# FFN weights loaded one pair of heads earlier, turned behind the last denominators and kept in SBUF; the first layer norm's scaling on ScalarE

## The chip, the core and the metric

The kernel runs on one core of a Trainium2 chip. The metric is the device time of one launch in microseconds. The engines are PE (matmuls), DVE (vector), ACT (scalar), POOL (GpSimd) and SP, whose queue issues all DMAs here. Each engine works through its own list of instructions in order and waits on semaphores.

## The reference

The input is x of 2 batches x 2048 rows x 256. All arithmetic is fp32.

```
x = x + attention(layernorm(x))          # 16 heads of 64; a key after the query gets score 1e-10, not minus infinity
x = x + ffn(layernorm(x))
ffn(h): for blk in 0..2:
    y = gelu(layernorm(linear(h, 2*blk)) * gamma + beta)
    h = linear(y, 2*blk + 1) + h
linear(x, l): x @ (dequant(q[l], scale[l]).T + (lora_b[l] @ lora_a[l]).T) + bias[l]
dequant(q, s) = (q / 7.5 - 1) * s, with one scale for each 16 columns
```

Masked keys keep a weight exp(1e-10 - max) in the softmax, so sums of the values and of the counts behind each query are added in (the `masked_...` names). There are six FFN weights of 256 x 256, each with a LoRA part of rank 32.

## The kernel before

Two programs follow each other, `attention` and `feed_forward`, each in its own block with a barrier between.

**Attention** goes over 16 pairs of heads in all (8 for each batch). A pair's scores are cut into NT = 20 tiles, each two blocks of 128 keys against a group of 512 queries, in groups 3, 2, 1, 0. For a tile, PE makes the scores of both heads (L794, L796, L799), ACT takes the exponential into `probs` (L988), PE multiplies with the values (`weighted`, L815), and the exponentials are added up in `acc` for the denominators: by POOL in all pairs but the last (L649, L656), by DVE in the last (`add_last`, L1108 and L1114), since POOL has the FFN weights to dequantise there. `probs` has three slots, so ACT's exponential of tile t waits until tile t - 3 has been added. After a group, PE sums `acc` over partitions (`denominators`, L765; group 0 straight from `probs`, L771), ACT copies the row out, and a chain of small DMAs and DVE operations inverts and spreads it (`take_den`, `invert`, `put_inverse`, `spread_inverse`, `normalise`, `store_heads`). Each group's result goes to DRAM.

PE's order has 6 slots a tile, 120 a pair. In the slots of pair i lies the background work for pair i + 1: projections, the scores for the row maxima with their reductions on DVE, and transposes. Constants such as `FIN`, `MAX_AT`, `XN_AT`, `TURN_AT`, `LORA_AT`, `WEIGHT_AT` say at which slot of the pair each piece stands, the same numbers on PE, ACT and DVE. The background pieces share three PSUM banks (`ps_bg`) in the order of `background`.

**The layer norm of x** is done in four chunks of 512 rows. For the first batch it stands at the program's start, for the second in the slots of pair 6 (`next_batch`, pairs counted from 0): DVE takes the statistics (`row_stats`), POOL raises the variance to -0.5 (`invert_root`, L567), DVE subtracts and multiplies in place in `xs` (`standardise`, L1149, four instructions of 128x256 a chunk), PE turns the chunk (`turn_x`, L703), ACT copies it back (`take_x`).

**The FFN weights** are loaded in the last pair (`load_ffn_weights`, L361 to L370, 14 DMAs into the buffers of `split`, `xs` and `w_in`, which are free by then); SP comes to it after the store of pair 14's last group. POOL dequantises them (`dequantise`, L604 and L607) behind its work for group 3. PE turns lora_b at the slots LORA_AT (24, 35, ... 79) and the weight at WEIGHT_AT (30, 41, ... 85) of the last pair (`turn_lora` L713, `turn_weight` L725 and L729), ACT copies both out (L949, L954), and SP stores six turned weights to DRAM, from where `feed_forward` loads them again (L1328) between its other loads.

**feed_forward** takes eight chunks of 512 rows in rounds of two. It starts with the output projection of the first two chunks by pieces (`heads_out_by_piece`, L1449), as their loads land. PE waits for the weights and biases only at `first_linear(0, 0)`.

## Time and profile before

| | us |
|---|---|
| median of 3 runs | 2405.03 |
| fastest, slowest run | 2403.07, 2453.09 |
| the profiled execution | 2412.48 |
| its span, first to last instruction | 2410.7 |

| engine | busy us | share of the span |
|---|---|---|
| PE | 2252.3 | 93% |
| DVE | 1426.4 | 59% |
| POOL | 1258.3 | 52% |
| ACT | 812.6 | 34% |

The attention block takes 2046.5 us of the span, the FFN block the rest. The busy share is an average over stages; a matmul's duration depends on the granted clock, which is at 2.4 GHz (1.00) or 1.2 GHz (0.50). The mean over the execution is 0.97. PE is furthest below that share in the first 100 us, in pair 6, in pair 15 and at the change between the two blocks.

### The profile page before, as it was taken

What the parts mean: (1) busy time and instruction counts of PE and PEld (TensorE: products, weight loads), DVE (VectorE), ACT (ScalarE), POOL (GpSimd) and SP (SyncE); (2) the same over time, 40 slices, a digit from 0 to 9 for tenths busy, and PEclk for the clock granted to TensorE, in tenths of its full rate; (3) what the DMA queues carried; (4) which work ended last, traced back from release to release, by engine and by line L of the source; (5) the groups of instructions that cost most, each with busy time, mean ns of one, the idle gap of its engine ahead of it and who ended that gap; (6) DMA issues with size and microseconds to landing.
All of it is one profiled execution on the core that took longest, in us unless ns stands there. A gap on an engine that the chain in (4) does not pass through costs nothing. (4 is left out here: it accounts for less than half of the span.)

```text
span 2410.7 us, 30473 instructions
## 1 busy us (share of the span) xinstructions
PE 2252.3 (93%) x10080; PEld 1148.3 (48%) x10080; DVE 1426.4 (59%) x3778; ACT 812.6 (34%) x1170; POOL 1258.3 (52%) x1151
## 2 busy tenths in 40 slices
PE   6999999999999988999999999999999976899987
PEld 2344444444444434444444444444444433767764
DVE  6765656565656575665556556565656533365664
ACT  1234343443433433343434343434343422011111
POOL 2275757575748473667666767575757420111110
PEclk9699999999999999999999999999999988999998
DMA  5545353535353543635353535444443412621100
GB/s 128 120 97 139 97 139 97 148 89 152 88 154 89 149 111 87 145 88 149 90 146 95 141 107 130 114 123 120 116 127 103 119 49 72 221 88 62 62 18 18
DMA packets 201979, 264.17 MB, mean 110 GB/s; under 512 B 68896, under 2 KB 85472, under 8 KB 201824
## 3 DMA queue, kind: packets, MB, share of 16 engines
q1 hardware_dynamic: 201824, 262.23, 41.5%
q8 instruction: 82, 1.34, 0.2%
q14 instruction: 73, 0.60, 0.1%
HBM read 171.44 MB, written 90.44 MB: 109 GB/s over the span
## 5 line engine op out<-in xcount | busy, mean ns | idle before, releaser
L656 POOL TENSOR_TENSOR acc<-acc,probs 128x512 f32<-128x512 f32 (+1 forms) x900 | 981.0, 1126 | 393.7 <-ACT probs L988 393.6
L988 ACT ACTIVATE probs<-ps_s 128x1024 f32<-128x1024 f32 (+2 forms) x640 | 549.1, 897 | 312.5 <-PE ps_s L796 148.5
L1048 DVE TENSOR_REDUCE partial<-ps_bg 128x1 f32<-128x512 f32 x768 | 490.3, 683 | 207.6 <-PE ps_bg L738 207.2
L794 PE MATMUL ps_s<-qq,kk 128*128 128x512 f32 (+3 forms) x1280 | 576.6, 451 | 21.4 <-ACT probs L988 21.4
L815 PE MATMUL ps_o<-probs,v 128*64 128x512 f32 (+3 forms) x2560 | 541.8, 544 | 0.0
L796 PE MATMUL ps_s<-qm,kl 128*128 128x512 f32 (+3 forms) x1280 | 470.1, 367 | 0.0
L686 PE MATMUL ps_bg<-xs,w_in 128*128 128x512 f32 x768 | 365.1, 599 | 9.8 <-DVE split L1025 8.5
L794 PEld LDWEIGHTS ps_s<-qq,kk 128*128 128x128 f32 x1280 | 245.5, 192 | 206.2 <-issue 157.8
L738 PE MATMUL ps_bg<-k_bf,q_bf 64*128 64x512 bf16 (+3 forms) x1280 | 276.3, 366 | 29.2 <-DVE split L1025 10.4
L1045 DVE CUSTOM_DVE_ANT_0 junk<-ps_bg,mask_q 128x512 bf16<-128x512 f32 (+3 forms) x512 | 230.8, 485 | 103.8 <-issue 102.7
L815 PEld LDWEIGHTS ps_o<-probs,v 128*64 128x64 f32 x2560 | 155.9, 137 | 231.7 <-issue 207.5
L796 PEld LDWEIGHTS ps_s<-qm,kl 128*128 128x128 f32 x1280 | 244.9, 191 | 38.8 <-issue 21.5
L738 PEld LDWEIGHTS ps_bg<-k_bf,q_bf 64*128 64x128 bf16 x1280 | 74.3, 93 | 364.8 <-issue 295.1
L906 ACT ACTIVATE split<-ps_bg,bias 128x512 fp32r<-128x512 f32 x128 | 88.0, 687 | 425.6 <-PE ps_bg L686 425.6
L649 POOL TENSOR_TENSOR acc<-probs 128x512 f32<-128x512 f32 x90 | 113.3, 1281 | 224.7 <-ACT probs L988 224.7
L1025 DVE SCALAR_TENSOR_TENSOR split<-ps_bg,bias,split 128x512 fp32r<-128x512 f32 x128 | 94.6, 739 | 200.5 <-ACT split L906 199.5
L686 PEld LDWEIGHTS ps_bg<-xs,w_in 128*128 128x128 f32 x768 | 141.2, 190 | 118.3 <-issue 98.0
L1360 POOL TENSOR_TENSOR c_rstd<-c_var,c_minus_half 128x4 f32<-128x4 f32 x32 | 35.5, 1109 | 274.2 <-DVE c_var L1535 274.2
L625 POOL TENSOR_TENSOR masked_num<-v_from,e 128x512 f32<-128x512 f32 x64 | 75.9, 1187 | 133.4 <-DVE num L1072 131.8
L1080 DVE TENSOR_TENSOR total<-den_sq,masked_den 32x32 f32<-32x32 f32 x64 | 40.7, 637 | 147.5 <-DMA den_sq<-den_rows 147.5
L799 PE MATMUL ps_s<-never_above,ident_bf 128*128 128x128 bf16 x512 | 118.4, 231 | 0.0
L1508 ACT ACTIVATE c_yt<-c_ps,c_be,c_ga 128x512 f32<-128x512 f32 x48 | 33.6, 775 | 237.2 <-PE c_ps L1405 237.2
(107 smaller groups left out, 1812.3 us busy)
## 6 DMA issues: line engine op xcount, KB each, us to landing
high_and_low<-split SPq DMA_DIRECT2D x128, 512.0 KB, 5.8
qq<-high_and_low SPq DMA_DIRECT2D x64, 512.0 KB, 4.7
kk<-high_and_low SPq DMA_DIRECT2D x128, 256.0 KB, 5.5
qm<-high_and_low SPq DMA_DIRECT2D x64, 256.0 KB, 6.2
kl<-high_and_low SPq DMA_DIRECT2D x64, 256.0 KB, 6.7
e<-masked_weights SPq DMA_DIRECT2D x128, 128.0 KB, 3.0
scale<-inverse_sums SPq DMA_DIRECT2D x128, 128.0 KB, 2.9
heads_turned<-o_out SPq DMA_DIRECT2D x64, 256.0 KB, 3.2
```

What stands on the lines that cost most here:

```text
L649: g.tensor_tensor(acc[h][:, group % 2, :], pr[:, 0:CH], pr[:, CH:2 * CH], ALU.add).then_inc(added, 1)
L656: g.tensor_tensor(acc[h][:, group % 2, q0:q0 + w], acc[h][:, group % 2, q0:q0 + w], probs[h][:, probs_slot(i, t), at:at + w], ALU.add).the ...
L686: mm = pe.matmul(bank("proj", j, u), w_in[:, s, m, :], xs[:, c, s, :], start=(s == 0), stop=(s == halves - 1))
L738: pe.matmul(bank("max", j, n, h)[:, 0:w], q_bf[HEAD[h], qb * P:(qb + 1) * P], k_bf[HEAD[h], CH * u:CH * u + w], start=True, stop=True).the ...
L794: pe.matmul(out, kk[:, h, kb * P:(kb + 1) * P], qq[:, h, q], start=True, stop=False, skip_group_check=True)
L796: mm = pe.matmul(out, kl[:, h, kb * P:(kb + 1) * P], qm[:, h, q], start=False, stop=not diagonal, skip_group_check=True)
L799: mm = pe.matmul(ps_s[:, h, at:at + P], ident_bf[:, :], never_above[:, :], start=False, stop=True, skip_group_check=True)
L815: mm = pe.matmul(ps_o[64 * h:64 * h + 64, q0:q0 + w], v[:, kb, 64 * h:64 * h + 64], probs[h][:, probs_slot(i, t), at:at + w], start=first, ...
L988: nc.scalar.activation(probs[h][:, probs_slot(i, t), 0:width], ps_s[:, h, 0:width], ACT.Exp, scale=SCORE_SCALE).then_inc(p_ready, 1)
L1025: e.scalar_tensor_tensor(part[:, 2 * m + 1, :], bank("proj", j, u), bias[:, m:m + 1], part[:, 2 * m, :].bitcast(F32), ALU.add, ALU.subtrac ...
L1045: e.tensor_tensor_reduce(junk[:, k, 0:w], of, mask_q[:, CH - w:CH], 1.0, 3 * NEVER, ALU.add, ALU.max, to).then_inc(max_read, 1)
L1048: e.reduce_max(to, of, AX.X).then_inc(max_read, 1)
```

## The change

1. `load_ffn_weights` is called in pair 14 in place of pair 15, behind `keep_split(15, 0)`, with a further wait on `bf_ready`, and uses 6 DMAs in place of 14.
2. `turn_lora` and `turn_weight` leave the slots of the last pair and follow its last denominators on PE; `take_lora` and `take_weight` follow the copy of these denominators on ACT. The table of banks is changed to match.
3. The six turned weights are not stored and loaded again. `xs` becomes a view of `home`, a buffer that outlives attention, and `feed_forward` multiplies with it.
4. `standardise` moves from DVE to ACT, as `x * rstd + shift` with Identity. POOL makes `shift` = -mean * rstd by two more small instructions a chunk. `row_stats` now also waits for `xn_done` of two chunks before, since the statistics are in two buffers.

```diff
@@ -120,8 +120,6 @@
 N_LAYERS = 6
-LORA_AT = [24 + 11 * l for l in range(N_LAYERS)]
-WEIGHT_AT = [30 + 11 * l for l in range(N_LAYERS)]
@@ -140,9 +138,10 @@
                 order += [("ln", (i + 2) // n_pairs, c) for c in PROJ_CHUNKS if TURN_AT[c] == n]
-            if i == n_pairs_in_all - 1:
-                order += [("lora", 0, l) for l in range(N_LAYERS) if LORA_AT[l] == n]
-                order += [("weight", 0, l) for l in range(N_LAYERS) if WEIGHT_AT[l] == n]
+    order.append(("lora", 0, 0))
+    for l in range(N_LAYERS):
+        order += [("lora", 0, l + 1)] if l + 1 < N_LAYERS else []
+        order.append(("weight", 0, l))
     first, users = {}, []
@@ -195,7 +194,7 @@
         bias = sb("bias", [P, 3])
-        xs = sb("xs", [P, 4, halves, CH])
+        xs = home.rearrange("p (c s t) -> p c s t", c=4, s=halves)
         split = [sb(f"split{b}", [P, 4, CH], F32R) for b in range(2)]
@@ -361,18 +363,19 @@
                     sp.wait_ge(proj_done, START + NPROJ * N)
+                    sp.wait_ge(bf_ready, START + 4 * N)
                     for b in range(2):
                         sp.wait_ge(split_kept[b], START + 64 * N)
-                    for l in range(n_layers):
-                        sp.dma_start(w_q[l], qweights[l].rearrange("(h p) d -> p h d", p=P)).then_inc(ffn_w_loaded, 16)
-                        sp.dma_start(la_in[l], lora_a[l]).then_inc(ffn_w_loaded, 16)
+                    for b, of in enumerate((slice(0, 4), slice(4, n_layers))):
+                        n_of = of.stop - of.start
+                        sp.dma_start(split[b][:, 0:n_of].bitcast(I32).rearrange("p l (h d) -> p (l h) d", h=halves),
+                                     qweights[of].rearrange("l (h p) d -> p (l h) d", p=P)).then_inc(ffn_w_loaded, 16)
+                    sp.dma_start(xs[0:R, 3].rearrange("r s (u d) -> r (s u) d", d=D),
+                                 lora_a[0:4].rearrange("l r d -> r l d")).then_inc(ffn_w_loaded, 16)
+                    sp.dma_start(split[1][0:R, 2].bitcast(F32).rearrange("r (l d) -> r l d", d=D),
+                                 lora_a[4:n_layers].rearrange("l r d -> r l d")).then_inc(ffn_w_loaded, 16)
                     sp.dma_start(sc_in, w_scales.rearrange("l (h p) g -> p (l h) g", p=P)).then_inc(ffn_w_loaded, 16)
                     sp.dma_start(lb_in, lora_b.rearrange("l (h p) r -> p (l h) r", p=P)).then_inc(ffn_w_loaded, 16)
-
-                def store_ffn_weights(l):
-
-                    sp.wait_ge(wt_ready, START + l + 1)
-                    sp.dma_start(wt[l], w_t[l].rearrange("p (h d) -> p h d", h=halves)).then_inc(wt_stored, 16)
@@ -498,7 +501,7 @@
                         keep_split(i + 1, 0)
-                    if not more:
+                    if i + 2 == N:
                         load_ffn_weights()
@@ -517,9 +520,6 @@
                         install_max(i + 1, 3)
-                    else:
-                        for l in range(4):
-                            store_ffn_weights(l)
                     spread_masked(i, 0)
@@ -532,9 +532,6 @@
                         install_chunk(i + 1, 1)
-                    else:
-                        for l in range(4, n_layers):
-                            store_ffn_weights(l)
                     take_den(i, 1)
@@ -564,7 +560,11 @@
                     pool.wait_ge(var_done, START + n)
+                    g.tensor_scalar(minus_mean[:, n % 2], mv[:, n % 2, :, 0], -1.0, None, ALU.mult).then_inc(mean_done, 1)
                     g.tensor_tensor(rstd[:, n % 2], var_eps[:, n % 2], minus_half[:, :], ALU.pow).then_inc(rstd_done, 1)
+                    pool.wait_ge(mean_done, START + n)
+                    pool.wait_ge(rstd_done, START + n)
+                    g.tensor_tensor(shift[:, n % 2], minus_mean[:, n % 2], rstd[:, n % 2], ALU.mult).then_inc(shift_done, 1)
@@ -707,7 +707,7 @@
                     if l == 0:
-                        pe.wait_ge(ffn_w_loaded, START + 16 * (2 * n_layers + 2))
+                        pe.wait_ge(ffn_w_loaded, START + 16 * 6)
                     bank_read("lora", 0, l)
@@ -839,13 +839,6 @@
                                 turn_x(next_batch(i), c)
-                    if i == N - 1:
-                        for l in range(n_layers):
-                            if LORA_AT[l] == n:
-                                turn_lora(l)
-                        for l in range(n_layers):
-                            if WEIGHT_AT[l] == n:
-                                turn_weight(l)
@@ -890,6 +883,11 @@
                     between(i, SLOTS)
+                turn_lora(0)
+                for l in range(n_layers):
+                    if l + 1 < n_layers:
+                        turn_lora(l + 1)
+                    turn_weight(l)
@@ -931,6 +929,16 @@
+                def standardise(batch, c):
+
+                    n = ln_count(batch, c)
+                    b = n % 2
+                    act.wait_ge(shift_done, START + n)
+                    for t in range(4):
+                        last = nc.scalar.activation(chunk_rows[c][:, t, :], chunk_rows[c][:, t, :], ACT.Identity,
+                                                    bias=shift[:, b, t:t + 1], scale=rstd[:, b, t:t + 1])
+                    last.then_inc(xn_done, 1)
+
                 def take_x(batch, c):
@@ -953,12 +961,16 @@
+                standardise(0, 3)
+                standardise(0, 2)
                 take_x(0, 3)
                 act.wait_ge(w_loaded, START + 144)
+                standardise(0, 1)
                 high(0, 0)
                     high(0, u)
+                standardise(0, 0)
                 take_x(0, 1)
@@ -999,14 +1011,16 @@
                             for c in PROJ_CHUNKS:
+                                if next_batch(i) is not None and XN_AT[c] == n:
+                                    standardise(next_batch(i), c)
                                 if next_batch(i) is not None and TURN_AT[c] == n:
                                     take_x(next_batch(i), c)
-                            for l in range(n_layers):
-                                if i == N - 1 and LORA_AT[l] == n:
-                                    take_lora(l)
-                                if i == N - 1 and WEIGHT_AT[l] == n:
-                                    take_weight(l)
                 evacuate(N - 1, "den", 0, fin_before(N - 1, NFIN))
+                take_lora(0)
+                for l in range(n_layers):
+                    if l + 1 < n_layers:
+                        take_lora(l + 1)
+                    take_weight(l)
@@ -1131,6 +1145,8 @@
                     dve.wait_ge(xs_loaded[c], START + 16 * (batch + 1))
+                    if n >= 3:
+                        dve.wait_ge(xn_done, START + n - 2)
                     for t in range(4):
@@ -1140,30 +1156,13 @@
-                def standardise(batch, c):
-
-                    n = ln_count(batch, c)
-                    b = n % 2
-                    dve.wait_ge(rstd_done, START + n)
-                    for t in range(4):
-                        last = e.tensor_scalar(chunk_rows[c][:, t, :], chunk_rows[c][:, t, :], mv[:, b, t, 0:1],
-                                               rstd[:, b, t:t + 1], ALU.subtract, ALU.mult)
-                    last.then_inc(xn_done, 1)
-
-                for c in (3, 2):
-                    row_stats(0, c)
-                    standardise(0, c)
+                row_stats(0, 3)
+                row_stats(0, 2)
                 dve.wait_ge(w_loaded, START + 144)
+                row_stats(0, 1)
                 low(0, 0)
-                row_stats(0, 1)
-                low(0, 1)
-                standardise(0, 1)
-                low(0, 2)
-                low(0, 3)
                 row_stats(0, 0)
-                low(0, 4)
-                standardise(0, 0)
-                for u in range(5, NPROJ):
+                for u in range(1, NPROJ):
                     low(0, u)
@@ -1232,7 +1229,7 @@
         wo = sb("c_wo", [P, n_pairs, D])
-        w = sb("c_w", [P, 2 * n_blk, halves, D])
+        w = home[:, 0:2 * n_blk * halves * D].rearrange("p (l h d) -> p l h d", l=2 * n_blk, h=halves)
         b_out_row = sb("c_b_out_row", [P, D])
@@ -1282,8 +1279,6 @@
         loads = []
-        for l in range(2 * n_blk):
-            loads.append((w[:, l], wt[l]))
         for k in range(n_blk):
```

**PE, the last pair, at slot 24.** `ps_s` are scores, `ps_o` the weighted values, `w_in` holds lora_b here. Before:

```order
L815 MATMUL ps_o<-probs,v 64x256 x2
L815 MATMUL ps_o<-probs,v 64x128 x2
L794 MATMUL ps_s<-qq,kk 128x512
L796 MATMUL ps_s<-qm,kl 128x512
L713 MATMUL ps_bg<-ident,w_in 32x128 x2
L794 MATMUL ps_s<-qq,kk 128x512
L796 MATMUL ps_s<-qm,kl 128x512
```

The first lora matmuls stand between the two halves of a tile's scores. In the change this row, and all others of L713, L725 and L729 in the pair, are gone from there.

**PE, the end of attention.** `split` holds the dequantised weights; L771 are the last denominators. Of the change:

```order
L771 MATMUL ps_bg<-probs,ones 64x128 x2
L713 MATMUL ps_bg<-ident,w_in 32x128 x4
L725 MATMUL ps_bg<-ident,split 128x128 x4
L729 MATMUL ps_bg<-split,home 128x256 x2
L713 MATMUL ps_bg<-ident,w_in 32x128 x2
L725 MATMUL ps_bg<-ident,split 128x128 x4
L729 MATMUL ps_bg<-split,home 128x256 x2
```

Two loras, then a weight and a lora by turns, six of each in all, and only then PE leaves the block.

**ACT, pair 6.** `home` is `xs`. Of the change, from the exponential of tile 11 on:

```order
L1000 ACTIVATE probs<-ps_s 128x1024 x2
L938 ACTIVATE home<-home,shift,rstd 128x256 x4
L1000 ACTIVATE probs<-ps_s 128x896 x2
L915 CAST rows<-ps_bg 8x128
L926 ACTIVATE rows<-rows 8x128
L929 ACTIVATE rows<-rows,masked_bias 8x128
L938 ACTIVATE home<-home,shift,rstd 128x256 x4
L1000 ACTIVATE probs<-ps_s 128x384 x2
L950 COPY home<-ps_bg 128x512 x2
```

Each chunk's four Identity instructions now stand in front of a tile's exponentials.

## Rows read from the trace of the kernel before

**Rows 1.** Busy time by stretch, pairs 5 and 6: us, busy of each engine (instructions), PEclk, DMA share, GB/s.

```profile
693.00:810.00 117.00, 114.86 (x528) 53.75 (x526) 72.07 (x191) 45.75 (x66) 77.99 (x71) 1.00 0.46 118
811.00:955.00 144.00, 127.13 (x560) 60.10 (x556) 96.53 (x247) 50.13 (x73) 82.66 (x75) 0.93 0.45 114
```

**Rows 2.** Timeline of PE, pair 15: start, duration, operation [idle before, releaser].

```profile
1942.52 1.06 PE L713 MATMUL ps_bg<-ident,w_in 128*32 128x128 f32 x4 [18.26 <-DMA w_in<-in_L_ffn_lora_b]
...
1949.83 1.05 PE L725 MATMUL ps_bg<-ident,split 128*128 128x128 f32 x8
...
1951.87 0.50 PE L794 MATMUL ps_s<-qq,kk 128*128 128x512 f32 x1
...
1957.32 0.50 PE L794 MATMUL ps_s<-qq,kk 128*128 128x512 f32 x1 [1.37 <-ACT probs L988]
...
1961.25 1.16 PE L725 MATMUL ps_bg<-ident,split 128*128 128x128 f32 x8
```

**Rows 3.** Timeline of SP's queue, pair 15.

```profile
1937.15 1.37 SPq L370 DMA_DIRECT2D w_in<-in_L_ffn_lora_b  x1
```

**Rows 4.** Busy time by stretch, behind the wait for the load.

```profile
1942.00:1950.00 8.00, 7.48 (x22) 3.78 (x23) 2.47 (x3) 2.41 (x3) 7.12 (x8) 0.59 0.02 5
1960.00:1970.00 10.00, 8.31 (x35) 4.54 (x31) 3.20 (x6) 2.43 (x3) 0.00 (x0) 0.83 0.00 0
```

**Rows 5.** Timeline of DVE, pair 15.

```profile
1930.25 3.56 DVE L1114 TENSOR_TENSOR acc<-acc,probs 128x256 f32<-128x256 f32 x8
1947.53 4.28 DVE L1114 TENSOR_TENSOR acc<-acc,probs 128x512 f32<-128x512 f32 x4 [13.71 <-ACT probs L988]
1958.21 2.50 DVE L1114 TENSOR_TENSOR acc<-acc,probs 128x512 f32<-128x512 f32 x4 [6.39 <-ACT probs L988]
```

**Rows 6.** Timeline of POOL, pair 15.

```profile
1928.27 1.26 POOL L625 TENSOR_TENSOR masked_num<-v_from,e 128x512 f32<-128x512 f32 x1 [1.61 <-DMA e<-masked_weights]
1942.55 0.62 POOL L604 TENSOR_SCALAR split<-split 128x512 f32<-128x512 int32 x1 [13.02 <-DMA w_in<-in_L_ffn_lora_b]
...
1953.40 1.06 POOL L607 TENSOR_TENSOR split<-split,w_in 128x512 f32<-128x512 f32 x1
```

**Rows 7.** Timeline of PE, the last work of attention.

```profile
2026.21 2.32 PE L771 MATMUL ps_bg<-probs,ones 128*64 128x512 f32 x16
```

**Rows 8.** Timeline of SP's queue, the change of blocks.

```profile
2039.96 0.33 SPq L459 DMA_DIRECT2D heads_turned<-o_out  x1
2046.53 0.39 SPq L1310 DMA_DIRECT2D c_wo<-in_L_attn_W_output  x1
```

**Rows 9.** DMA issues: count, KB each, median us to landing.

```profile
heads_turned<-o_out SPq DMA_DIRECT2D x64, 256.0 KB, 3.2
```

**Rows 10.** Timeline of ACT, the last pair and pair 6.

```profile
2007.00 0.59 ACT L954 COPY xs<-ps_bg 128x512 f32<-128x512 f32 x1 [2.81 <-PE ps_bg L729]
...
935.80 0.88 ACT L988 ACTIVATE probs<-ps_s 128x384 f32<-128x384 f32 x2
```

**Rows 11.** Timeline of PE, pair 6.

```profile
897.51 0.60 PE L738 MATMUL ps_bg<-k_bf,q_bf 64*128 64x512 bf16 x1 [6.59 <-DVE partial L1048]
...
902.01 1.11 PE L738 MATMUL ps_bg<-k_bf,q_bf 64*128 64x512 bf16 x2 [1.76 <-DVE partial L1048]
...
925.17 1.11 PE L703 MATMUL ps_bg<-ident,xs 128*128 128x128 f32 x4 [3.80 <-DVE partial L1045]
```

**Rows 12.** Timeline of DVE, pair 6.

```profile
887.37 9.17 DVE L1080 TENSOR_TENSOR total<-den_sq,masked_den 32x32 f32<-32x32 f32 x1
...
919.83 5.06 DVE L1149 TENSOR_SCALAR xs<-xs,mv,rstd 128x256 f32<-128x256 f32 x4
```

**Rows 13.** Timeline of POOL, pair 6.

```profile
887.18 9.31 POOL L656 TENSOR_TENSOR acc<-acc,probs 128x512 f32<-128x512 f32 x8
```

**Rows 14.** The inversion's first operation over the whole span: duration ns min/median/max.

```profile
L1080 DVE TENSOR_TENSOR total<-den_sq,masked_den x64: 171/180/9167, 173.5 to 2032.8; 32x32 f32<-32x32 f32 x64
```

**Rows 15.** Timeline of PE, the program's start.

```profile
38.45 0.98 PE L703 MATMUL ps_s<-ident,xs 128*128 128x128 f32 x7 [3.43 <-DVE xs L1149]
```

More of the change, by code:

```diff
@@ L213, in attention @@
         rstd = sb("rstd", [P, 2, 4])
+        minus_mean = sb("minus_mean", [P, 2, 4])
+        shift = sb("shift", [P, 2, 4])
         qq = sb("qq", [P, 2, S], F32R)
@@ L1194, in _ @@
                                 row_stats(next_batch(i), c)
-                            if next_batch(i) is not None and n == XN_AT[c]:
-                                standardise(next_batch(i), c)
                         if i == N - 1 and n % 6 == 1 and n // 6 <= LAST_TILE[1]:
@@ L1618, in program @@
     inverses = nc.dram_tensor("inverse_sums", [2, 2, CH], F32).ap()
[L1619 to L1621 removed]
+    with nc.sbuf_tensor("home", [P, 4 * halves * CH], F32) as home_tensor:
+        home = home_tensor[:, :]
+        attention(nc, x, [w_query, w_key, w_values], [b_query, b_key, b_values], (qweights, scales, lora_a, lora_b),
+                  parts, max_kept, kept, inverses, ot, home)
+        feed_forward(nc, x, ot, home, w_output.rearrange("n h e -> (n h) e"), b_output, biases, ln_gamma, ln_beta, y)
 _INS = ["L0_attn_residual", "L0_attn_W_key", "L0_attn_W_query", "L0_attn_W_values", "L0_attn_W_output",
```

16 lines of the change are left out of this document (6 added, 10 removed).

## The prediction

> **What bounds the kernel now.** The page's busy times come first: PE works 93% of the span, so what counts is where PE stands still or runs at the low clock. The busy times by stretch then show that the pairs of heads are alike but for two. Pair 5 needs 117.0 us between its neighbours' last denominators, pair 6, with the second batch's layer norm in it, 144.0, and PE is busy in nearly all of pair 5 but idle for 16.9 us of pair 6, and at a mean clock of 0.93 [rows 1]. The last pair lasts as long as the others though it has no projections and no maxima to make. PE's timeline tells why: 18.26 us at slot 24, waiting for lora_b [rows 2], because SP reaches the loads only behind the store of pair 14's last group, and the last of them is issued at 1937.15 [rows 3]. The timelines of DVE and POOL say what would have been late without that wait [rows 5, 6]. The chain that ends last runs through the FFN block on PE and tells nothing of these places.
>
> **Part 1: the earlier load.** The issues move to pair 14, at about slot 36. SP then waits there for the last stores of `split`, and behind it queue the spreads for group 1, the installs for the next pair, and the denominators of group 3 at slot 60. Fewer DMAs than now, and none of those behind has a reader on PE within 20 slots. I cost it at nothing; if the stores land late, SP is late by some 6 us for work that has about that much room. The wait of 18.3 us goes.
>
> **Part 2: turning leaves the last pair.** A lora takes PE 1.06 us at the low clock, so 0.6 at full with what it breaks up, and a weight 2.04 (1951.87 - 1949.83) [rows 2]; six of each are 15.8. ACT's copies stand in its queue ahead of exponentials, and PE waits for these four times behind them, 0.36 to 1.69 us and 4.0 in all; 1.37 is one [rows 2]. After the long wait PE runs at the low clock of 1.2 GHz up to about 1949, and again between 1960 and 1970 [rows 4]: (1 - 0.59) x 8 = 3.3 and (1 - 0.83) x 10 = 1.7 us of full-clock work, less what is idle, say 4.4. The sum on PE is 18.3 + 15.8 + 4.0 + 4.4 = 42.5 us.
>
> **What is late next: DVE's sums.** In the last pair DVE makes the sums for the denominators, and the wait for the load hides two delays. First, the normalisation of pair 14's last group holds DVE until 1930.25, with the eight additions of tiles 3 and 4 queued behind it: they start there, as one row [rows 5]. Second, POOL dequantises from 1929.5 on, when its masked part ends, since the weights are there by then; that takes 11.9 us (1942.55 to 1954.46) [rows 6]. While both work, an addition takes DVE 1.07 us (4.28 for four) in place of 0.63 (2.50 for four) [rows 5]. So DVE adds tiles 3, 4 and 5 from 1930.25 to about 1943.1 (12 x 1.07), tiles 6 and 7 to 1948.1 (8 x 0.63), and then takes the numerator of group 3, 0.7, which PE needs before it may multiply tile 8. Unhindered, PE would be there at 1941.1 (3.93 a tile: 1961.25 - 1957.32 [rows 2]). It is held for 7.7 us, in three or four pieces, since exponentials wait for the slots too. From there on DVE needs 2.5 us a tile and PE 3.9, and PE leads again. These waits may drop the clock for a while: 1.3. The last pair gains 42.5 - 7.7 - 1.3 = 33.5 us. The ends: 42.5 if DVE gets by unharmed, 28 if the low clock lasts over the rest of the group.
>
> **The tail.** From the last denominators (end 2028.5) [rows 7] to the FFN's first DMA (2046.5) [rows 8] there are 18.0 us in which PE has nothing to do. The last store is issued at 2039.96 and needs 3.2 us [rows 8, 9], so 3.3 us lie between its landing at 2043.2 and the new block. The turning now stands there: 15.8 us on PE and the last copy of 0.59 on ACT [rows 10], to about 2045.0, if the clock stays up, as it may since PE does not stop in between. That is 1.8 us behind the store's landing: cost 1.8. Between 0 (the 3.3 us have slack) and 17 (all at 1.2 GHz: 31.6 + 0.6 - 14.7).
>
> **Part 3: no store and reload.** The reload stands on SP's queue behind the pieces that PE needs first, and PE asks for weights only in its first linear layer, 2098, when all have landed. Zero; its cover is the output projection of two chunks.
>
> **Part 4: scaling on ACT.** In pair 6 there are two separate losses. One is the scaling itself: four instructions of DVE take 5.06 us, since POOL adds at the same time, and PE waits 3.80 for them [rows 11, 12]; with the low clock after it (7 us at half rate with PE busy for 5.2: 2.6) and small waits of 1.6, some 8 us. On ACT this is gone. The other is an inversion, `total`, of 0.18 us that takes 9.17 [rows 12, 14]: it starts 0.2 us after POOL begins eight additions, which end with it [rows 13]. PE waits 6.59 and 1.76 [rows 11], and the low clock for 13.7 us costs 3.6 more: 12. The change doesn't touch this instruction, but POOL now has minus_mean and shift round each power. The trace has no such instruction of four columns; those of 512 take 0.62 and 1.06 [rows 6], so the two cost 0.1 to 1.7 us a chunk, and I take 0.4, since nearly all of a row's time there is columns. Two chunks stand before these additions, which start 0.8 us later, and `total` comes while POOL is at small work. I take it that it slips in: it did 63 times of 64. The cost is four more ACT instructions a chunk ahead of an exponential: about 0.4 each by the narrowest rows (0.88 for two of 384 columns) [rows 10], 1.6 a chunk, in gaps of ACT that are mostly longer; zero to 1.6 for one chunk. I take 20 us for pair 6; ends 6 and 23.
>
> ScalarE is slower at this by the Trainium skill ("ScalarE: Activation LUTs", Rules for kernel authors), which says to use VectorE for add and mul, and gives about 0.3 us an instruction and 0.83 ns an element. An estimate by it is 0.51 us each, 2.05 a chunk; no trace here has the Identity form of 256 columns. By it the sum would lose at most 2 us more over all of pair 6.
>
> At the start PE loses a wait of 3.43 [rows 15], caused by a memset of POOL that held DVE's scaling. The memset now meets DVE's casts instead, and the first chunk's copy queues behind the second's scaling on ACT, up to 2.7 later. Zero, from 3 gained to 3 lost.
>
> **Sum.** 33.5 - 1.8 + 20 = 51.7. The profiled execution, 2412.5, would be 2360.8. The median stands 7.5 below it, so 2353.3. Some of these 7.5 may be the starved inversion, if other executions don't have it; I put the median at 2355.
>
> **The rivals.**
>
> A. The inversion is an accident of the profiled execution, or stays starved: then 12 us of the gain are missing, 2365. For it: once in 64 [rows 14], and the 7.5 between profile and median. Against: the order of instructions is fixed and pair 6 is where POOL adds longest without rest. Chance 0.25.
>
> B. DVE does not bind in the last pair, since its additions slip between POOL's instructions more cheaply: 7 to 9 us more gain, 2347. Chance 0.14.
>
> C. The turning is exposed: PE falls to 1.2 GHz behind the last denominators and the copies on ACT alternate with it. 15 us more than in the sum, 2370. For it: after every long wait in these rows the clock is low [rows 4]. Against: there is no wait before this work. Chance 0.12.
>
> D. Slower than before. ACT now stops in pair 6 until POOL has made `shift`, and POOL's queue has additions ahead of it that need ACT's exponentials. If ACT comes to slots 70, 76, 88 and 100 before POOL has passed the additions ahead of tiles 10, 11, 13 and 15, each stop lasts POOL's backlog, up to 9.3 [rows 13], and PE follows at the low clock for as long, which costs half of it again: 4 x 14.0 = 56 in place of a gain of 20, 2355 + 76 = 2431. It decides whether POOL is behind ACT by more than a tile. Against: the slots lie one to four tiles behind POOL's power. Chance 0.03.
>
> E. The change does not do what it says: SP is late in pair 14 and PE waits for the loads or installs after all, most of 18 us: 2372. Chance 0.03.
>
> My forecast has 0.43. The **range** for 8 in 10: from 2334 (B with the start's gain and no exposed tail) to 2376 (A with C's first half, or with the low clock lasting in the last pair). Within 2% of 2405.0 is down to 2356.9, about what a measurement of this kernel can tell from no change. The forecast's own width puts six tenths of it below that line, B wholly, A for a fifth, C hardly: faster 0.52, within 0.45, slower 0.03 (D is mostly under 2% and larger only if the stops add up).
>
> **What would show it.** Right: no wait for a load in pair 15; waits of PE for ACT and of ACT for DVE's additions near tiles 5 to 8 there; about 2 us more between the last store's landing and the new block; pair 6 at about 124 us with no `total` over 1.2 us. Wrong: PEclk near 0.5 behind the last denominators, ACT's Identity rows with idle time put down to POOL, or a last pair below 82 us.

## The result, and the profile after

The changed kernel takes **2487.45 us** (median of 5 runs, 2486.26 to 2501.57) against 2405.58 of the kernel before (5 runs, 2403.07 to 2453.09): ratio 1.033, 95% interval 1.031 to 1.036. It is 3.3% slower, where 2.1% faster was forecast. Its profiled execution took 2501.57 us, span 2499.7. Here and in the table below, medians are of all executions, while the ratios leave out those more than 1.5% above a kernel's fastest.

The two stretches that the change was made for did get shorter. Busy time by stretch, changed kernel, pair 6 and the last pair (columns as in [rows 1]):

```profile
870.80:999.00 128.20, 121.48 (x569) 57.76 (x564) 81.62 (x234) 58.82 (x94) 83.92 (x83) 1.00 0.50 128
2029.50:2113.20 83.70, 77.39 (x380) 39.40 (x377) 53.75 (x87) 36.11 (x45) 22.45 (x17) 0.98 0.20 59
```

Pair 6 needs 128.2 us (145.3 before, from the end of a pair's last denominators to the next such end) and the last pair 83.8 (119.4). No wait for a load is left in it. But pairs that the change doesn't touch got longer, here pair 5, which took 118.5 before, measured from end to end (the stretch of 117.0 in [rows 1] leaves a piece out):

```profile
742.70:870.80 128.10, 120.75 (x538) 55.97 (x534) 78.37 (x191) 47.23 (x70) 77.89 (x71) 0.96 0.43 111
```

PE is idle for 7.3 us of it and has a mean clock of 0.96. The waits of PE name the cause by its line. Columns: who waited for whom, us in total, times, longest. First before, then after:

```profile
PE ps_bg L738 <- DVE partial L1048: 9.3, 5, 6.6
```

```profile
PE ps_bg L738 <- DVE partial L1062: 76.9, 18, 5.3
```

DVE is late with the row maxima (`partial`), because of what stands ahead of them. The timeline of DVE in pair 0, before:

```profile
172.32 1.29 DVE L1048 TENSOR_REDUCE partial<-ps_bg 128x1 f32<-128x512 f32 x2 [0.90 <-PE ps_bg L738]
173.53 1.10 DVE L1080 TENSOR_TENSOR total<-den_sq,masked_den 32x32 f32<-32x32 f32 x1
174.66 0.34 DVE L1084 RECIPROCAL inverse<-total 32x32 f32<-32x32 f32 x1
```

and after, with POOL's timeline beside it:

```profile
172.26 1.29 DVE L1062 TENSOR_REDUCE partial<-ps_bg 128x1 f32<-128x512 f32 x2 [0.90 <-PE ps_bg L738]
173.46 7.90 DVE L1094 TENSOR_TENSOR total<-den_sq,masked_den 32x32 f32<-32x32 f32 x1
181.39 0.34 DVE L1098 RECIPROCAL inverse<-total 32x32 f32<-32x32 f32 x1
...
171.99 9.33 POOL L656 TENSOR_TENSOR acc<-acc,probs 128x512 f32<-128x512 f32 x8
```

`total` adds two buffers of 32x32 and takes 1.10 us before and 7.90 after. It starts in the second of POOL's eight additions and now ends at 181.36, when the last of them ends (171.99 + 9.33 = 181.32). PE, at 182.34, has waited:

```profile
182.34 0.60 PE L738 MATMUL ps_bg<-k_bf,q_bf 64*128 64x512 bf16 x1 [5.33 <-DVE partial L1062]
```

POOL's additions end there because it has run out of work. PE's wait also holds up the scores, ACT gets none to turn into exponentials, and POOL's next addition waits for these:

```profile
187.63 2.23 POOL L656 TENSOR_TENSOR acc<-acc,probs 128x256 f32<-128x256 f32 x4 [6.32 <-ACT probs L1000]
```

What that does to the clock is in the busy times of the same stretch, before and after:

```profile
182.00:186.00 4.00, 4.00 (x23) 2.52 (x24) 3.78 (x8) 1.94 (x2) 2.49 (x5) 1.00 0.18 66
186.00:198.00 12.00, 11.91 (x64) 5.51 (x62) 7.82 (x30) 5.23 (x8) 9.15 (x9) 1.00 0.62 155
```

```profile
182.00:186.00 4.00, 3.66 (x13) 2.05 (x13) 2.42 (x5) 1.45 (x4) 0.00 (x0) 0.50 0.18 65
186.00:198.00 12.00, 11.94 (x54) 5.83 (x53) 8.48 (x24) 3.18 (x5) 4.76 (x6) 0.79 0.23 67
```

Behind the wait the granted clock is 0.50, then 0.79, where it was 1.00. So this is the inversion of [rows 12 to 14], which the kernel before held once, in pair 6. All its instances over the span (as [rows 14]), and the page's row, with busy time and mean ns; the last row is the page of before:

```profile
L1094 DVE TENSOR_TENSOR total<-den_sq,masked_den x64: 170/266/7896, 173.5 to 2117.9; 32x32 f32<-32x32 f32 x64
...
L1094 DVE TENSOR_TENSOR total<-den_sq,masked_den 32x32 f32<-32x32 f32 x64 | 131.1, 2049 | 137.0 <-DMA den_sq<-den_rows 137.0
```

```profile
L1080 DVE TENSOR_TENSOR total<-den_sq,masked_den 32x32 f32<-32x32 f32 x64 | 40.7, 637 | 147.5 <-DMA den_sq<-den_rows 147.5
```

One by one, 14 of the 64 take 7.9 us: that of group 3 in every pair but pair 6 and the last. Thirteen of these pairs last 126.6 to 131.9 us, 128.8 on average, and pair 0 ends 9.2 later than before (226.6, 217.4). Before, the same thirteen took 119.0 on average, so the loss is 9.8 times 13 and 9.2, some 137 us, against 17.1 and 35.6 gained in pair 6 and the last pair.

### The profile page after: what moved, and what is told of

It is laid out like the page before. It is cut to its first block and busy times, and to the rows that moved or that the text cites. A ratio compares the mean times of both kernels' runs of the same rounds, so it can differ in the third digit from the quotient of the medians.

```text
span 2499.7 us, 30484 instructions
## 1 busy us (share of the span) xinstructions
PE 2303.1 (92%) x10080; PEld 1168.9 (47%) x10080; DVE 1501.8 (60%) x3746; ACT 829.8 (33%) x1202; POOL 1266.5 (51%) x1167
## 5 line engine op out<-in xcount | busy, mean ns | idle before, releaser
L794 PE MATMUL ps_s<-qq,kk 128*128 128x512 f32 (+3 forms) x1280 | 588.2, 460 | 21.4 <-ACT probs L1000 21.4
L815 PE MATMUL ps_o<-probs,v 128*64 128x512 f32 (+3 forms) x2560 | 554.9, 555 | 3.3 <-DVE num L1086 3.3
L796 PE MATMUL ps_s<-qm,kl 128*128 128x512 f32 (+3 forms) x1280 | 478.6, 374 | 0.0
L686 PE MATMUL ps_bg<-home,w_in 128*128 128x512 f32 x768 | 371.3, 608 | 13.8 <-DVE split L1039 10.8
L738 PE MATMUL ps_bg<-k_bf,q_bf 64*128 64x512 bf16 (+3 forms) x1280 | 287.7, 378 | 97.5 <-DVE partial L1062 76.9
L794 PEld LDWEIGHTS ps_s<-qq,kk 128*128 128x128 f32 x1280 | 253.0, 198 | 216.7 <-issue 166.5
L796 PEld LDWEIGHTS ps_s<-qm,kl 128*128 128x128 f32 x1280 | 253.5, 198 | 40.7 <-issue 22.7
L1094 DVE TENSOR_TENSOR total<-den_sq,masked_den 32x32 f32<-32x32 f32 x64 | 131.1, 2049 | 137.0 <-DMA den_sq<-den_rows 137.0
L686 PEld LDWEIGHTS ps_bg<-home,w_in 128*128 128x128 f32 x768 | 143.0, 193 | 123.7 <-issue 101.1
L799 PE MATMUL ps_s<-never_above,ident_bf 128*128 128x128 bf16 x512 | 124.0, 242 | 0.0
```

What stands on the lines that cost most here:

```text
L686: mm = pe.matmul(bank("proj", j, u), w_in[:, s, m, :], xs[:, c, s, :], start=(s == 0), stop=(s == halves - 1))
L738: pe.matmul(bank("max", j, n, h)[:, 0:w], q_bf[HEAD[h], qb * P:(qb + 1) * P], k_bf[HEAD[h], CH * u:CH * u + w], start=True, stop=True).the ...
L794: pe.matmul(out, kk[:, h, kb * P:(kb + 1) * P], qq[:, h, q], start=True, stop=False, skip_group_check=True)
L796: mm = pe.matmul(out, kl[:, h, kb * P:(kb + 1) * P], qm[:, h, q], start=False, stop=not diagonal, skip_group_check=True)
L799: mm = pe.matmul(ps_s[:, h, at:at + P], ident_bf[:, :], never_above[:, :], start=False, stop=True, skip_group_check=True)
L815: mm = pe.matmul(ps_o[64 * h:64 * h + 64, q0:q0 + w], v[:, kb, 64 * h:64 * h + 64], probs[h][:, probs_slot(i, t), at:at + w], start=first, ...
```

## The experiments

**Held** below means an inversion above 5 us in the profiled execution. The chips differ, so every kernel stands beside the kernel before on its own chip. For the other executions the number held is not on record. The theory was that the two inputs of `total` in SBUF can be kept from DVE by POOL's additions. The first rival was that the new POOL instructions or buffers of the change do it, the second that the longer pairs have another cause.

| kernel | chip | median us (range, runs) | before there | held |
|---|---|---|---|---|
| before | A | 2405.6 (2403.1 to 2453.1, 5) | | 1 |
| after | A | 2487.5 (2486.3 to 2501.6, 5) | 2405.6 | 14 |
| e1_pad64 | B | 2441.7 (2413.6 to 2477.5, 10) | 2441.8 (2411.4 to 2505.8, 31) | 3 |
| e2_scale_on_act | B | 2428.1 (2404.3 to 2467.1, 10) | same | 6 |
| e3_weights_only | B | 2429.7 (2409.0 to 2474.7, 10) | same | 10 |
| e4_after_invert70 | B | 2441.1 (2428.6 to 2454.3, 10) | same | 8 |
| f1_before_one_input | C | 2407.6 (2401.8 to 2410.6, 10) | 2430.5 (2412.1 to 2455.3, 15) | 0 |
| f2_after_one_input | C | 2360.7 (2359.3 to 2364.2, 6) | same | 0 |
| f3_after_again | C | 2483.5 (2462.8 to 2502.1, 4) | same | 14 |
| f4_after_delay | C | 2486.7 (2483.6 to 2490.1, 4) | same | 14 |
| g1_before_home | D | 2444.7 (2428.7 to 2459.9, 10) | 2466.2 (2430.8 to 2493.3, 19) | 4 |
| g2_after_sums_two_inputs | D | 2470.1 (2437.3 to 2480.0, 10) | same | 11 |
| g3_one_input_act | D | 2389.3 (2387.2 to 2390.9, 4) | same | 0 |
| g4_one_input_weights | D | 2371.0 (2368.1 to 2375.6, 4) | same | 0 |
| h1_before_all_moved | E | 2534.9 (2513.1 to 2549.2, 4) | 2416.0 (2411.3 to 2440.1, 7) | 15 |
| h2_after_pool_drains | E | 2365.4 (2359.4 to 2368.5, 4) | same | 0 |
| h3_after_small_last | E | 2381.8 (2373.3 to 2590.4, 4) | same | 4 |
| h4_after_third | E | 2490.3 (2473.3 to 2494.6, 4) | same | 14 |

**Which part of the change starts it?** Four kernels on chip B. In the kernel before, 64 unused bytes:

```diff
         rstd = sb("rstd", [P, 2, 4])
+        pad = sb("pad", [P, 16])
```

> The kernel before with one unused buffer of 64 bytes a partition behind rstd, so that qq and all behind it, acc, den_sq and total among them, lie 64 bytes higher, as in the change. Theory P (placement): group 3's inversion is now held for some 7.9 us in nearly every pair, the pairs last about 128 us, and the time is near 2405 + 13 x 9 = 2520. Theory I (the instructions ahead on POOL and DVE decide): nothing moves, 2405, and the inversion takes 1.1 us in 15 pairs.

The second has of the change only part 4, the scaling on ACT (its lines of the diff above):

> The kernel before with the scaling of the layer norm on ACT alone (with minus_mean and shift, POOL's two further instructions, and row_stats' wait); the FFN weights as before. Theory P: held in nearly every pair as far as the 64 bytes are the cause, 2405 - 17 + 120, near 2510. Theory I, with POOL's small instructions as the cause: the same 2510. If neither buffers nor POOL's instructions are it, 2388.

The third is the changed kernel with the scaling back on DVE:

> The change with the scaling left on DVE as before: only the loads one pair earlier, the turning behind the last denominators, and xs in a buffer that stands ahead of all others. Theories P and I: the inversion passes as before, the last pair gains about 35, the tail costs 2: near 2372. If the new place of xs or the other list of instructions for the weights is the cause, near 2490.

The fourth moves group 3's inversion two slots:

```diff
-INVERT_SLOT = {3: 68, 2: 106, 1: 118, 0: SLOTS + 8}
+INVERT_SLOT = {3: 70, 2: 106, 1: 118, 0: SLOTS + 8}
```

> The change with group 3's inversion at slot 70 in place of 68 on DVE. If the held inversion is the whole loss, the pairs fall back to about 119 us and the time to 2487 - 13 x 9 = 2370 or below. If it is held there too, the time stays near 2487. If other waits would take its place, the pairs lie between.

None of them singled a part out, and e1, e2 and e3 took none of the times expected of them, as the kernel before itself takes 2441.8 on this chip. Their ratios to before are 1.000 (0.995 to 1.005), 0.996 (0.990 to 1.001), 0.999 (0.994 to 1.004) and 1.002 (0.998 to 1.006). Held inversions occur in all of them, and executions of one kernel lie up to 94 us apart. (A ratio near 1 does not say that e2 and e3 lose nothing. Without held inversions the same parts take 2389.3 and 2371.0, g3 and g4 below, on another chip, so e2 lies 39 us above its own and e3 59; the kernel before lies 34 above the 2407.6 of f1.) e1 and e3 have neither minus_mean nor shift on POOL, so POOL's new instructions are not needed for a hold. Two slots later a hold is shorter and as long as what is left of POOL's run. DVE's timeline, then POOL's, of e4:

```profile
174.88 5.29 DVE L1094 TENSOR_TENSOR total<-den_sq,masked_den 32x32 f32<-32x32 f32 x1
...
170.79 9.34 POOL L656 TENSOR_TENSOR acc<-acc,probs 128x512 f32<-128x512 f32 x8
```

It ends at 180.17, POOL's run at 180.13.

**Is it the two inputs, and what is the change worth without it?** `total` becomes one reduction over a view that has both terms, in both kernels; slot and waits stay:

```diff
-        masked_den = sb("masked_den", [32, 2, 4, 2, 16])
+        sums = sb("sums", [32, 9, 2, 16])
+        masked_den = sums[:, 0:8].rearrange("p (a g) h e -> p a g h e", a=2)
...
-        den_sq = sb("den_sq", [32, 2, 16])
+        den_sq = sums[:, 8]
...
-                    e.tensor_tensor(total[:, :, :], den_sq[:, :, :], masked_den[:, i % 2, group], ALU.add
+                    m = 4 * (i % 2) + group
+                    e.tensor_reduce(total[:, :, :].rearrange("p h e -> p (h e)"),
+                                    sums[:, m:9:8 - m].rearrange("p k h e -> p (h e) k"), AX.X, ALU.add
                                     ).then_inc(total_ready, 1)
```

> The kernel before, with `total` made by one tensor_reduce over a view that has both terms, instead of a tensor_tensor of two inputs in SBUF. Same slot, same waits, same place among POOL's additions. Theory (two SBUF inputs need a path that POOL's unbroken additions keep from DVE): no `total` above 0.6 us, pair 6 at 132 to 136 us, every other pair but the last at 118 to 121, median 2390 to 2400 and no steps of 9 us between executions. Rival (anything of DVE's that arrives there is held, whatever its inputs): the reduce is held 7.9 to 9.2 us in 1 to 6 pairs, as before.

> The changed kernel with the same edit of `total`. Theory: no `total` above 0.6 us, all pairs but the last and pair 6 at 118 to 121 us, the last pair 84 to 88, pair 6 at 124 to 128, median 2340 to 2365. Then the change by itself is worth 35 to 55 us and the loss was the held inversions alone. Rival 1 (anything of DVE's is held there): 2430 to 2490, pairs at 127 to 131. Rival 2 (the longer pairs come from something else that the change does, such as buffers that moved, and the held inversion only goes with them): no long `total`, but pairs still at 123 us or more.

The unchanged kernel and one with a small delay ran beside them:

```diff
+        late = sb("late", [32, 4])
...
+                    e.memset(late[:, :], 0.0)
                     e.tensor_tensor(total[:, :, :], den_sq[:, :, :], masked_den[:, i % 2, group], ALU.add
```

> The changed kernel as it is, beside the others on their chip. If whether the inversion is held is settled by a few nanoseconds, and differs between chips and executions: anything from 2360 to 2490, in steps of some 9 us, with as many pairs at 124 to 131 us as there are held inversions. If it is the program alone that settles it: 14 held inversions and 2480 to 2500 here too.

> The changed kernel with one small memset of DVE (32x4, some 60 ns) ahead of each `total`, which then comes that much later into POOL's additions. If the moment of arrival decides: another number of held inversions than in the changed kernel on the same chip, by at least 4 of 16, either way, at some 9 us each in the time. If it doesn't: the same number within 2, and a time within 20 us of it.

All instances in f2, in the view of [rows 14], f1's being alike:

```profile
L1096 DVE TENSOR_REDUCE total<-sums x64: 198/207/213, 172.1 to 1978.2; 32x32 f32<-32x64 f32 x64
```

With one input it takes 0.20 to 0.22 us everywhere, at the same place among POOL's additions, and the scatter shrinks to 5 us in f2 and 9 in f1. f2 is 46.9 us under f1, and their ranges are 38 us apart. Against the kernel before, f2's ratio is 0.972 (0.966 to 0.977), f1's 0.991 (0.988 to 0.995). f1's median came out 8 above the 2400 expected, and pair 6 was longer than expected in both: 140.7 in f1 (132 to 136 expected), 132.6 in f2 (124 to 128). The delay told nothing of the moment of arrival: `total` and the memset both start where the reduction before them ends, so `total` came hardly later.

```profile
171.03 1.29 DVE L1063 TENSOR_REDUCE partial<-ps_bg 128x1 f32<-128x512 f32 x2 [0.90 <-PE ps_bg L739]
172.25 7.88 DVE L1096 TENSOR_TENSOR total<-den_sq,masked_den 32x32 f32<-32x32 f32 x1
172.26 0.06 DVE L1095 MEMSET late<- 32x4 f32 x1
```

**Controls and parts.** g1 moves xs to `home` in the kernel before, g2 has f2's buffers with the old addition, g3 and g4 are e2 and e3 with one input.

```diff
-        xs = sb("xs", [P, 4, halves, CH])
+        xs = home.rearrange("p (c s t) -> p c s t", c=4, s=halves)
```

> The kernel before, with nothing but the place of `xs` (and of c_w) changed: both are views of `home`, allocated ahead of the two programs, as in the changed kernel. Every buffer of attention behind it moves in SBUF; no instruction does. If the place of the buffers decides whether the inversion is held: 10 or more held inversions of 16, and 2460 to 2500. If it doesn't: a few held inversions as in the kernel before, ratio 0.99 to 1.01.

> The control for the kernel with one tensor_reduce: the changed kernel with den_sq and masked_den in the one buffer `sums`, but `total` still a tensor_tensor of two inputs. If it is the two inputs that are held: inversions of 7.9 us again, 8 or more of 16, 2430 to 2500. If the new place of the two buffers had done it: none, and 2355 to 2365.

> The kernel before with `total` as one tensor_reduce and of the change only the scaling on ACT. By the terms of the prediction without the inversion: pair 6 at 132 to 134 in place of 140.7, nothing else, so 2397 to 2401. If ACT's stops behind POOL cost something (rival D): pair 6 above 145, over 2410.

> The kernel before with `total` as one tensor_reduce and of the change only the weights' part. By the terms of the prediction: last pair 33.5 shorter at 86, 1.8 lost behind it, so 2374 to 2377. If the turning at the end costs more (rival C): above 2385. The sum of this gain and the scaling's should be that of the two together, 46.9 us (2407.6 - 2360.7), within 3.

g2's row on its page, with f2's places and two inputs:

```profile
L1095 DVE TENSOR_TENSOR total<-sums 32x32 f32<-32x32 f32 x64 | 107.3, 1677 | 135.0 <-DMA sums<-den_rows 135.0
```

Eleven are held again, so it was the inputs and not the place that freed f2. Two of its pairs show, too, that the moment of arrival doesn't decide. First pair 2, held, then pair 3, which got by; `total` starts 1.47 us behind the start of POOL's run in both:

```profile
425.07 9.33 POOL L657 TENSOR_TENSOR acc<-acc,probs 128x512 f32<-128x512 f32 x8
426.54 7.90 DVE L1095 TENSOR_TENSOR total<-sums 32x32 f32<-32x32 f32 x1
...
552.10 11.58 POOL L657 TENSOR_TENSOR acc<-acc,probs 128x512 f32<-128x512 f32 x12
553.57 1.10 DVE L1095 TENSOR_TENSOR total<-sums 32x32 f32<-32x32 f32 x1
```

g1 is like the kernel before or better (0.991, 0.987 to 0.995): in that kernel and on that chip `home` alone adds nothing. (Its expectation says that every buffer behind `xs` moves. That was wrong. In the built programs only `w_in`, `bias` and the constants ahead of `xs` move, up by 16,384 bytes, and `xs` down by 8,000.) The terms where nothing is held would be: scaling 18.3 us (2407.6 - 2389.3), weights 36.6 (2407.6 - 2371.0). Both kernels are faster than was expected of them (2397 to 2401, 2374 to 2377), and the terms don't add up to the 46.9 of both within the 3 expected: 54.9. But f1 and f2 ran on another chip than g3 and g4, so these two differences are not shown to be the terms.

The kernels without a held inversion also give the price of one. In the eleven profiled executions with three or more (h3's, at a clock of 0.834, left out), the time above the median of the kernel with the same parts and nothing held (f1, f2, g3 or g4) is 8.5 to 10.4 us for each.

**Why nearly always in the changed kernel?** Its layout has both moves at once: that of g1, and all buffers behind `rstd` 64 bytes higher, as in e1. h1 has both, in the kernel before; h3 has only the first, in the changed kernel, since `minus_mean` and `shift` are allocated last there; h2 keeps the layout and lets POOL pause between additions.

```diff
 h1, on top of g1:
+        minus_mean = sb("minus_mean", [P, 2, 4])
+        shift = sb("shift", [P, 2, 4])
 h2, on top of the change:
-                                pool.wait_ge(added, START + POOL_OPS * i + n - 1)
+                                pool.wait_ge(added, START + POOL_OPS * i + n)
```

> The kernel before with every buffer of attention exactly where the changed kernel has it: `xs` and c_w in `home`, and two unused buffers in the places of minus_mean and shift. No instruction differs. If this layout (which neither part alone has) makes the inversion be held in nearly every pair: 11 or more of 16, and 2480 to 2500. If the layout has no part in it: as many as in the kernel before on this chip, ratio 0.985 to 1.015.

> The changed kernel, `total` with its two inputs, but each of POOL's additions waits until the one before it has ended, where it waited for the last but one. POOL's run then has small gaps. If DVE is held because POOL's additions overlap and never let go: no `total` above 1.5 us, all pairs at 118 to 121, 2358 to 2375. If a run of additions holds DVE however they follow one another: 7.9 us and more as before, and 2450 to 2510.

> The changed kernel with minus_mean and shift allocated last, so that the buffers behind them lie 64 bytes lower. If the layout decides: another number of held inversions than in the changed kernel on this chip, by 4 or more. If it doesn't: the same within 3, time within 25 us.

> The changed kernel again, as the control for the other three on this chip: 11 to 14 held inversions, 2460 to 2500, as on the two chips so far.

h1 is the clearest run of all. It executes the instructions of the kernel before and is 119 us slower (1.048, 1.041 to 1.055), more than the 2480 to 2500 expected. All instances, then pair 6 on DVE and POOL:

```profile
L1082 DVE TENSOR_TENSOR total<-den_sq,masked_den x64: 173/180/9139, 176.7 to 2166.8; 32x32 f32<-32x32 f32 x64
...
944.26 9.14 DVE L1082 TENSOR_TENSOR total<-den_sq,masked_den 32x32 f32<-32x32 f32 x1
...
944.05 9.30 POOL L658 TENSOR_TENSOR acc<-acc,probs 128x512 f32<-128x512 f32 x8
```

All 15 pairs in which POOL adds are held. h3 goes the other way (0.984, 0.980 to 0.989): three of its four executions took 2373.3 to 2383.6 us, 13 to 23 above f2, by the price above an estimated one to three holds. (The fourth, the profiled one, has a mean clock of 0.834, so its pairs of 128 us say nothing here, and its four holds of 6.8 to 6.9 us are no count for the others.) h4, the changed kernel on the same chip, is at 2490 again. On this chip the layout decides.

h2 takes POOL's overlap away and no inversion is held. Its instances, `total` in pair 0, and POOL's run from there:

```profile
L1094 DVE TENSOR_TENSOR total<-den_sq,masked_den x64: 169/180/1298, 171.8 to 1975.0; 32x32 f32<-32x32 f32 x64
...
171.85 0.73 DVE L1094 TENSOR_TENSOR total<-den_sq,masked_den 32x32 f32<-32x32 f32 x1
...
171.25 11.52 POOL L656 TENSOR_TENSOR acc<-acc,probs 128x512 f32<-128x512 f32 x9
```

In the kernel before the same nine additions, without pauses, take 10.02:

```profile
172.06 10.02 POOL L656 TENSOR_TENSOR acc<-acc,probs 128x512 f32<-128x512 f32 x9
```

POOL pays 1.5 us for nine, has the time, and the kernel takes 2365.4 (0.978, 0.975 to 0.982) with `total` as it was. (`total` also comes elsewhere here, 0.60 us into POOL's first addition instead of 0.23 into the second.)

So both f2 and h2 beat the two kernels; f2 has the lowest median, 2360.7.

## Why the prediction was wrong

**The step that failed** is in part 4: "I take it that it slips in: it did 63 times of 64". For pair 6 that came true: `total` takes 0.17 us there in the profile of after (rows below). What failed is that the sum put the same instruction of the other pairs at nothing. I read [rows 14] as one accident in 64. Only 15 of the 64 inversions meet POOL's additions in a run of eight or more, that of group 3 in each pair but the last, and each of these can be held: h1 holds all 15. Before, the other 14 waited 1.10 us, until one addition of POOL ended, and got by there. The maximum of [rows 14] was seen and its price worked out (12 us), but only for pair 6, and rival A let it stay or go, never multiply. In its place came 14 holds of 7.9 us, some 137 us. Two hints were there before. `total` at 1.10 us in pair 0, where its minimum is 0.17, means that it had been waiting for POOL there too. And the slowest run before, 2453.1, was 50 us above the fastest; at the price of a hold found above that is an estimated five of them.

**What tipped it** was no instruction of the change but its places in SBUF, which the prediction costed at nothing and didn't mention. Shown: with h1 the layout alone does it, with h3 most of it goes when 64 bytes are taken back, and f2 and h2, with the changed kernel's layout (f2 but for `sums`), hold nothing. For h1 and h3 this is one chip; the changed kernel itself held 14 in its profile on each of three.

**The rest, step by step**, is read where nothing is held, from f1 to f2 on one chip. Busy time by stretch, pair 6 and the last pair, f1 and then f2:

```profile
809.20:949.90 140.70, 126.75 (x570) 59.97 (x565) 92.16 (x250) 51.09 (x78) 82.42 (x75) 0.95 0.46 116
1897.90:2017.60 119.70, 97.20 (x476) 52.03 (x474) 49.18 (x87) 40.55 (x57) 16.84 (x17) 0.90 0.26 71
```

```profile
806.70:939.30 132.60, 125.95 (x568) 59.63 (x564) 80.49 (x234) 58.88 (x94) 83.34 (x83) 0.96 0.49 124
1886.60:1973.50 86.90, 80.34 (x380) 40.63 (x378) 54.38 (x87) 36.15 (x45) 22.42 (x17) 0.94 0.20 57
```

- Part 1, the earlier load at no cost: right. Pair 14 has 118.2 us in f2, and no wait for a load is left in the last pair, so rival E is out. Part 3, zero forecast: from its first DMA on the FFN block takes 364.2 us before and 364.7 after. The start, zero forecast: pair 0 ends at 216.9 in f1 and 215.9 in f2.
- Part 2, the last pair: 33.5 forecast, 32.8 measured (119.7 - 86.9), 35.6 in the profile of after. That DVE's sums would be late next, against rival B, was right too. ACT's timeline of after, the longest and a usual one of five such waits (15.4 us together):

```profile
2053.71 1.94 ACT L1000 ACTIVATE probs<-ps_s 128x1024 f32<-128x1024 f32 x2 [5.34 <-DVE acc L1128]
2058.67 1.94 ACT L1000 ACTIVATE probs<-ps_s 128x1024 f32<-128x1024 f32 x2 [3.03 <-DVE acc L1128]
```

- The tail: 1.8 forecast, 3.5 measured. The last denominators of PE, the last copy of ACT, SP's last store and its first load of the new block, after:

```profile
2111.18 2.32 PE L771 MATMUL ps_bg<-probs,ones 128*64 128x512 f32 x16
...
2129.61 0.59 ACT L962 COPY home<-ps_bg 128x512 f32<-128x512 f32 x1 [1.56 <-PE ps_bg L729]
...
2124.28 0.34 SPq L462 DMA_DIRECT2D heads_turned<-o_out  x1
2135.02 0.42 SPq L1305 DMA_DIRECT2D c_wo<-in_L_attn_W_output  x1
```

  From 2113.5 to 2135.0 are 21.5 us, 18.0 before. The turning ends at 2130.2, 2.7 behind the store's landing at 2127.5 (2124.3 + 3.2 [rows 9]). Rival C is out: the granted clock stays at 1.00 behind the last denominators:

```profile
2112.00:2120.00 8.00, 8.00 (x55) 5.67 (x52) 1.92 (x5) 2.82 (x7) 0.00 (x0) 1.00 0.24 85
2120.00:2128.00 8.00, 8.00 (x49) 6.06 (x50) 0.69 (x1) 2.65 (x6) 0.00 (x0) 1.00 0.17 66
```

- Part 4, pair 6: 20 forecast, of which 8 for the scaling and 12 for the inversion, but 12.7 measured. The scaling gave 8.1 (140.7 - 132.6). The inversion by itself was worth 4.6 (145.3 - 140.7), since the two losses overlap and were added up as if they didn't: in f1, with `total` at 0.20, the scaling of another chunk stands where it stood, slow beside POOL's additions, and PE waits for that. DVE, then PE of f1:

```profile
887.01 4.93 DVE L1152 TENSOR_SCALAR xs<-xs,mv,rstd 128x256 f32<-128x256 f32 x4
...
894.62 1.12 PE L739 MATMUL ps_bg<-k_bf,q_bf 64*128 64x512 bf16 x2 [5.40 <-DVE partial L1049]
```

  The changed kernel's own pair 6, with nothing held, takes 128.2 us at a mean clock of 1.00; f2's 132.6 are at 0.96, with 4.5 us more of busy time on PE for the same work (125.95, 121.48). Why the clock differs is not known.

- ACT's new work in the profile of after, four scalings; then POOL's three small instructions for the next chunk, with `total` among them:

```profile
943.84 2.06 ACT L938 ACTIVATE home<-home,shift,rstd 128x256 f32<-128x256 f32 x4
...
945.47 0.25 POOL L563 TENSOR_SCALAR minus_mean<-mv 128x4 f32<-128x4 f32 x1
945.66 1.06 POOL L564 TENSOR_TENSOR rstd<-var_eps,minus_half 128x4 f32<-128x4 f32 x1
946.63 0.17 DVE L1094 TENSOR_TENSOR total<-den_sq,masked_den 32x32 f32<-32x32 f32 x1
946.87 0.20 POOL L567 TENSOR_TENSOR shift<-minus_mean,rstd 128x4 f32<-128x4 f32 x1
```

  2.06 a chunk, where I took 1.6 and the estimate by the Trainium skill ("ScalarE: Activation LUTs", Rules for kernel authors) was 2.05. The trace agrees with the page, which was nearer than my rows. ACT is also the slower engine at this, as the page has it, though it compares them in bf16: the median instruction takes 0.59 us on ACT and took 0.41 on DVE. The two new POOL instructions take 0.45 a chunk, for which I took 0.4. Rival D didn't come: g3 with the scaling on ACT has pair 6 at 132.6.

Together: the forecast was 2355, f2 takes 2360.7. That is partly luck. From the profile of before to that of f2 the last pair, pair 6 and the tail give 32.5 + 12.7 - 3.5 = 41.7 us where 51.7 was forecast. The other pairs are 9.7 shorter in all, which no part of the forecast had, and 6.5 of it is there in f1 as well, that is without the change. So the forecast fits a kernel without this hold, its terms less well, and it was wrong for the one that was run. The loss of 127 us between f2 and the changed kernel (2487.5 - 2360.7, on two chips; 2483.5 - 2360.7 on one) is the held inversion, as undoing it in two independent ways shows.

**Open:** why these places in SBUF decide. The two moves together hold it nearly always on one chip. In the kernel before, either alone didn't raise the number on the chips where it was tried, but e1 and g1 never ran on the chip of h1, e3 with `home` alone had ten held in its profile on chip B, and the chips differ for one and the same kernel (before: 2405.6 to 2466.2). Nothing here shows how it is settled who gets in. It isn't the moment of arrival (g2's pairs 2 and 3). Nor does every run hold it: in the profiles of kernels with two inputs and POOL's additions back to back, 23 inversions of other groups met a run with 3.7 to 4.5 us left, and all got by within 1.25 us.

The Trainium skill ("SBUF — State Buffer", SBUF: two separate sides) has DVE and GpSimd share one pair of ports, which a DVE instruction with two SBUF inputs needs against a GpSimd one that reads SBUF; whichever starts first has it for its whole instruction. The 1.10 us before and the 0.20 of one input agree with that. The 7.90, which runs on over six more instructions of POOL behind the one that it met, does not.

## What to carry to other kernels

A maximum far above the median in a group of equal instructions is not an accident until the trace says how many of them met the same condition: count those that could have been held, not all of the group, and price the case in which all of them are. Executions of one kernel that lie several such waits apart (2403 and 2453 us here, before the change) are the same warning. Keep small DVE additions of two SBUF inputs out of an unbroken run of POOL's additions, or give them one input. Here that cost 0.03 us an instruction (0.20 for 0.17), held nothing in four kernels, and brought the executions of one kernel to within 4 to 9 us of each other.

## What the runs showed of the hardware that was not expected

- A DVE addition of 32x32 elements with two inputs in SBUF takes 0.17 us alone, 1.10 when it waits for one addition of POOL, and 5.3, 7.9 or 9.2 when it waits to the end of POOL's run. The same sum as a reduction of one view takes 0.20 everywhere.
- With each of POOL's additions waiting for the one before, in place of back to back, nothing was held; the longest `total` was 1.30 us.
- Moving buffers by 64, 8,000 and 16,384 bytes, with no instruction changed, cost 119 us on one chip (2416.0 to 2534.9).
- Once held, `total` waits to the end of POOL's run, wherever it came into it (six more additions with 7.9 us, seven with 9.2, four with 5.3). In one program the outcome repeats: the changed kernel held 14 in each of three profiles, on three chips, f4 14 again and h1 all 15, while other programs close to them held 1 to 11.
